# A split user bias, a second layer norm by row factors through DRAM, and another passage and end of a GNN + LSTM kernel

## The reference, cut to what matters

```
xn  = layernorm(x)                                       # first norm, per user
h   = item_feat @ W_item.T + b_item                      # [N, H]
x1  = x + relu(adj @ h + xn @ W_user.T + b_user)         # adj is [N, N], 400 MB
z   = layernorm(x1)                                      # second norm, per user
hs  = LSTM over the N rows of z (one sequence)           # h, c start at zero
g   = argmax(hs @ W_lin.T + b_lin)                       # 0 or 1 per row
w   = g * hs; inc = cumsum(w)
out = x1 + 2*hs + (inc - w)*fw_att + (inc[-1] - inc)*bw_att
```

## Time and profile before

| | |
|---|---|
| median of 3 runs | 1447.24 us (1446.77 to 1447.74) |
| the profiled execution | 1444.94 us, its span 1443.1 us |
| busy share PE / DVE / ACT / POOL | 98% / 86% / 74% / 15% |
| the chain that ended last | PE 91%, DVE 3%, issue 2%, POOL 2%, DMA 1% |
| HBM read / written | 422.42 MB / 10.28 MB |
| stage 1, passage, stage 2, end begin at about | 0, 1136, 1149, 1419 us of the span |

### The profile page before, as it was taken

One profiled execution on the slowest core, in us unless ns is written; L12 is line 12 of the kernel. 1 busy time (PEld: TensorE's weight loads), 2 busy tenths in 40 slices (PEclk: granted clock), 3 DMA queues, 4 the chain that ended last, 5 costly groups with the idle time before them and its releaser, 6 DMA issues.

```text
span 1443.1 us, 26187 instructions
## 1 busy us (share of the span) xinstructions
PE 1412.8 (98%) x7478; PEld 1214.0 (84%) x7478; DVE 1242.8 (86%) x2052; ACT 1067.8 (74%) x1502; POOL 214.5 (15%) x193
## 2 busy tenths in 40 slices
PE   8999999999999999999999999999999899999994
PEld 7878888888888888888888888888888799999993
DVE  7998998998998999999989989989989666676667
ACT  6677777777877877877877877777777576556662
POOL 0000010010001001001001001000000132027775
PEclk9999999999999999999999999999999999999997
DMA  9999999999999999999999999999999203000003
GB/s 374 360 331 357 403 364 370 407 360 362 404 365 364 407 357 364 407 355 377 396 358 387 385 352 401 378 347 403 373 362 400 87 0 142 0 2 0 1 0 143
DMA packets 134877, 433.16 MB, mean 300 GB/s; under 512 B 18683, under 2 KB 35900, under 8 KB 134718
## 3 DMA queue, kind: packets, MB, share of 16 engines
q1 hardware_dynamic: 127776, 426.43, 78.0%
q10 hardware_dynamic: 7070, 6.34, 1.6%
HBM read 422.42 MB, written 10.28 MB: 300 GB/s over the span
## 4 chain that ended last, share of the span: by engine, by line
PE 91%; DVE 3%; issue 2%; POOL 2%; DMA 1%; ACT 0%; POOLq 0%; DVEq 0%; SPq 0%; ACTq 0%
PE psG L842 24%; PE psG L843 24%; PE psG L844 24%; PE psZ L965 8%; PE psZ L951 2%; PE psZ L953 2%; PE psZ L955 2%; PE psG L863 1%; PE psT L810 1%; PE psI L890 1%; DVE a_lo L1130 1%; POOL own L526 1%; PE psZ L971 1%; DMA raw<-in_adj_main 1%; POOL own L529 1%
## 5 line engine op out<-in xcount | busy, mean ns | idle before, releaser
L634 ACT ACTIVATE a_hi<-raw 128x1000 fp32r<-128x1000 f32 (+1 forms) x800 | 821.8, 1031 | 244.8 <-PE psG L844 208.4
L1130 DVE TENSOR_TENSOR a_lo<-raw,a_hi 128x1000 fp32r<-128x1000 f32 (+1 forms) x800 | 911.0, 1170 | 74.5 <-ACT a_hi L634 55.2
L842 PE MATMUL psG<-a_hi,item_hi 128*128 128x500 f32 x1560 | 620.5, 398 | 2.1 <-DVE a_lo L1130 1.1
L843 PE MATMUL psG<-a_lo,item_hi 128*128 128x500 f32 x1560 | 606.0, 388 | 0.0
L844 PE MATMUL psG<-a_hi,item_lo 128*128 128x500 f32 x1560 | 604.7, 388 | 0.0
L842 PEld LDWEIGHTS psG<-a_hi,item_hi 128*128 128x128 f32 x1560 | 293.5, 188 | 66.9 <-issue 5.6
L844 PEld LDWEIGHTS psG<-a_hi,item_lo 128*128 128x128 f32 x1560 | 293.2, 188 | 59.4
L843 PEld LDWEIGHTS psG<-a_lo,item_hi 128*128 128x128 f32 x1560 | 293.6, 188 | 58.6 <-issue 4.4
L452 POOL TENSOR_TENSOR rstd<-var,minus_half 125x4 f32<-125x4 f32 x40 | 76.1, 1902 | 1019.5 <-DVE var L1106 1019.5
L965 PE MATMUL psZ<-hist,wh 128*128 (+1 forms) x1264 | 167.8, 276 | 1.2 <-DVE hist L1304 1.1
L965 PEld LDWEIGHTS psZ<-hist,wh 128*128 128x128 f32 x1264 | 154.9, 192 | 1.7 <-issue 1.6
(11 more groups left out here) (174 smaller groups left out, 769.9 us busy)
## 6 DMA issues: line engine op xcount, KB each, us to landing
raw<-in_adj_main SPq DMA_DIRECT2D x760, 500.0 KB, 6.5
raw<-in_adj_main SPq DMA_DIRECT2D x40, 250.0 KB, 4.5
sq<-rstd_copy ACTq DMA_DIRECT2D x20, 250.0 KB, 7.1
x_copy<-xb SPq DMA_DIRECT2D x20, 250.0 KB, 7.1
u<-x_copy SPq DMA_DIRECT2D x1, 5000.0 KB, 14.4
out<-u SPq DMA_DIRECT2D x25, 200.0 KB, 2.4
u<-in_itemT SPq DMA_DIRECT2D x9, 512.0 KB, 10.1
xb<-in_xT SPq DMA_DIRECT2D x18, 250.0 KB, 5.9
```

The costliest lines, as they stand in the source:

```text
L634: nc.scalar.activation(a_hi[:, s % CUT, 0:n], raw[:, r % RAW, at:at + n], ACT.Copy)\
L842: pe.matmul(bank, w_hi, hi, start=(c == 0), stop=False)
L843: pe.matmul(bank, w_hi, lo, start=False, stop=False)
L1130: last = dve.tensor_tensor(a_lo[:, s % CUT, 0:m], raw[:, r % RAW, at:at + m], a_hi[:, s % CUT, 0:m].bitcast(f32), ALU.subtract)
```

## The change

- **Bias.** `wu` and `v` are split in high and low parts (fp32r); the bias becomes three matmuls like the others. ScalarE makes `v_hi` after piece 4, VectorE `v_lo` after piece 5, TensorE adds the bias after piece 7 (before: after piece 5). In block 0 the bias moves from piece 11 to 13 and the matmuls of `wx` from 12 to 7.
- **Second norm.** `normalise` and `to_columns` go. `add_relu` writes x1 to a buffer of its own, `x1b`, and the rows' 1/std and shift (`row_terms`) go to DRAM after piece 8 (`send_terms`), come back after piece 12 in two broadcasts of 250 KB (`spread_terms`, into `sq` and `un_bb`), and VectorE applies them in place to `x1b` after pieces 16 and 17. `out_u` reads `x1b` and moves from piece 10 to 18.
- **Waits of SP and VectorE.** The next x is loaded without waiting for the store of x1; `add_relu` waits for that store and for `out_u` of the block before.
- **Passage.** Eight matmuls of the identity (`KEEP_WARM`) follow the transposes; the first half of step 1 of the LSTM runs before the transposes back; the input matmuls of step 2 come before the second half of step 1.
- **End.** Two rows of x1 are copied to `x1_last` early; `total` comes before `last_y(1)`; ScalarE makes the shift in PSUM; 13 output parts of 400 to 1000 columns instead of 25; the check follows the last part; POOL's last base sum is issued before its wait for the gate.

```diff
-AT = dict(relu=1, x1=2, scaled=3, bias=5, rows2=3, stats2=4, pair2=5, eps2=5, scale2=6, norm2=7, back2=8, out2=10,
-          rows1=11, stats1=12, pair1=13, eps1=13, send=15, spread=19, store=7, load=10, wx=12)
-FIRST = dict(rows=0, stats=1, send=3, centre=3, centred=4, spread=6, scaled=9, bias=11)
+AT = dict(relu=1, x1=2, scaled=3, v_hi=4, v_lo=5, bias=7, rows2=3, stats2=4, pair2=5, eps2=5, scale2=7, send2=8, spread2=12, apply2=16, shift2=17, out2=18,
+          rows1=11, stats1=12, pair1=13, eps1=13, send=15, spread=19, store=7, load=10)
+FIRST = dict(rows=0, stats=1, send=3, centre=3, centred=4, spread=6, wx=7, scaled=9, v_hi=10, v_lo=11, bias=13)
+OUT_ENDS = (10, 20, 30, 40, 60, 80, 105, 130, 155, 180, 205, 230, K)
+POOL_OUTS = (3, 5, 8, 11)
 (SP)
-                        sp.wait_ge(x1_stored, 16 * j)
-                        sp.wait_ge(ln_rows, 2 * j + 1)
+                        sp.wait_ge(x1_ready, j)
 (ScalarE)
-            def normalise(count):
...
+            def send_terms(j):
+                act.wait_ge(ln_scale, j)
+                act.dma_start(rows_dram.rearrange("k (p s) -> p k s", s=SUB), row_terms[:, :, :])\
+                    .then_inc(terms_stored, 16)
+            def spread_terms(j):
+                act.wait_ge(terms_stored, 16 * j)
+                for k, t in enumerate((factors, rl)):
+                    act.dma_start(t[:, 0:BW], rows_dram[k:k + 1, :].to_broadcast([P, BW])).then_inc(terms_spread, 16)
+            def high_user(j):
+                act.wait_ge(v_ready, j + 1)
+                nc.scalar.activation(v_hi[:, :], v, ACT.Copy).then_inc(v_hi_ready, 1)
...
-                act.wait_ge(ln_back, count)
+                act.wait_ge(ln_applied, 2 * count)
 (TensorE)
-                        pe.wait_ge(v_ready, j + 1)
-                        pe.matmul(bank, wu[:, :], v[:, :], start=False, stop=False)
+                        pe.wait_ge(v_lo_ready, j + 1)
+                        pe.matmul(bank, wu_hi[:, :], v_hi[:, :], start=False, stop=False)
+                        pe.matmul(bank, wu_hi[:, :], v_lo[:, :], start=False, stop=False)
+                        pe.matmul(bank, wu_lo[:, :], v_hi[:, :], start=False, stop=False)
-                    if has2 and r == AT["back2"]:
-                        to_columns(j)
 (TensorE, passage)
+            for _ in range(KEEP_WARM):
+                pe.matmul(psG[:, 1, 0:P], ident[:, :], ident[:, :], start=True, stop=True)
+            from_state(1, 0, 0, 1)
...
             from_input_f32(1, 1, 1)
-            from_state(1, 0, 0, 1)
-            from_state(1, 1, 0, 1)
...
             from_input(LO_ONLY, 2, 0)
+            from_state(1, 1, 0, 1)
 (VectorE)
+            def low_user(j):
+                dve.wait_ge(v_hi_ready, j + 1)
+                dve.tensor_tensor(v_lo[:, :], v, v_hi[:, :].bitcast(f32), ALU.subtract).then_inc(v_lo_ready, 1)
             def add_relu(j):
...
-                dve.tensor_tensor(xb[:, j % 2, :], xb[:, j % 2, :], rl[:, :], ALU.add).then_inc(x1_ready, 1)
+                if not (isinstance(j, int) and j == 0):
+                    dve.wait_ge(x1_stored, 16 * j)
+                    dve.wait_ge(u_ready, j)
+                dve.tensor_tensor(x1b[:, :], xb[:, j % 2, :], rl[:, :], ALU.add).then_inc(x1_ready, 1)
+            def apply_rstd(j):
+                dve.wait_ge(terms_spread, 32 * j)
+                dve.tensor_tensor(by_s(x1b), by_s(x1b), by_r(factors[:, :]), ALU.mult)\
+                    .then_inc(ln_applied, 1)
+            def apply_shift(j):
+                dve.wait_ge(ln_applied, 2 * j - 1)
+                dve.tensor_tensor(by_s(x1b), by_s(x1b), by_r(rl[:, :]), ALU.add)\
+                    .then_inc(ln_applied, 1)
 (VectorE, end)
-            last_y(1)
             dve.wait_ge(cum_ready, 4)
             dve.scalar_tensor_tensor(total[:, :], cum[:, K:K + 1], -1.0, mbw[:, :], ALU.mult, ALU.mult)\
                 .then_inc(total_ready, 1)
+            last_y(1)
```

More of the change, by code:

```diff
@@ L151, in program @@
         xb = sb("xb", [P, 2, BW], f32, first)
-        v = sb("v", [P, BW], f32, first)
-        normed = sb("normed", [P, SUB * HID], f32, first)
+        v_hi = sb("v_hi", [P, BW], f32r, first)
+        v_lo = sb("v_lo", [P, BW], f32r, first)
+        x1_rows = sb("x1_rows", [P, SUB * HID], f32, first)
+        x1b = x1_rows[:, 0:BW]
+        wu = x1_rows[:, 0:HID]
+        item_tail = x1_rows[:, HID:HID + STACKED]
+        normed = x1_rows
         sq = sb("sq", [P, BW], f32, first)
@@ L193, in program @@
         own = sb("own", [P, 2, 2, K])
+        x1_last = sb("x1_last", [P, 2, K])
         x1_head = sb("x1_head", [P, L])
@@ L509, in write_y, with base, sums @@
                 pool.tensor_tensor(rows, own[:, par, :, :], run_c[:, par, :, :], ALU.add).then_inc(y_ready, 1)
-            def sums(i, par, reset=False):
+            def base(i, par):
+                rows = x1[:, :].rearrange("p (k l) -> p l k", l=L)[:, ds(2 * i, 2), :]
+                pool.tensor_tensor(own[:, par, :, :], hist[:, ds(2 * i, 2), :], rows, ALU.add).then_inc(base_ready, 1)
+            def sums(i, par, reset=False, last=False):
+                if last:
+                    pool.wait_ge(h_ready[0], W + 2 * i + 2)
+                    pool.wait_ge(h_ready[1], W + 2 * i + 2)
+                    pool.wait_ge(y_ready, i - 1)
+                    base(i, par)
                 pool.wait_ge(gated, i + 1)
@@ L524, in sums @@
                     write_y(i - 1, 1 - par)
-                rows = x1[:, :].rearrange("p (k l) -> p l k", l=L)[:, ds(2 * i, 2), :]
-                pool.tensor_tensor(own[:, par, :, :], hist[:, ds(2 * i, 2), :], rows, ALU.add).then_inc(base_ready, 1)
+                if not last:
+                    base(i, par)
                 pool.wait_ge(base_ready, i + 1)
@@ L545, in _ @@
                 sums(2 * i + 1, 1)
-            sums(PAIRS - 2, 0)
+            sums(PAIRS - 2, 0, last=True)
             pool.wait_ge(run_c_ready, PAIRS - 1)
@@ L652, in body @@
                         spread_rstd(0)
-                    if has2 and r == AT["norm2"]:
-                        normalise(j)
+                    if r == (FIRST if items else AT)["v_hi"]:
+                        high_user(j)
+                    if has2 and r == AT["send2"]:
+                        send_terms(j)
+                    if has2 and r == AT["spread2"]:
+                        spread_terms(j)
                     if has2 and r == AT["out2"]:
@@ new lines, in first_cell_tanh @@
+            def first_cell_tanh(g):
+                act.wait_ge(c_ready[g], 1)
+                nc.scalar.activation(tb(g, 3), group(C, g), ACT.Tanh, scale=0.5).then_inc(th_ready[g], 1)
+            first_gates(0)
+            first_cell_tanh(0)
+            act.wait_ge(ln_scale, NB)
+            for s in range(2):
+                nc.scalar.activation(normed[0:SW, s * HID:(s + 1) * HID], psT[0:SW, s * HID:(s + 1) * HID],
+                                     ACT.Identity, bias=shift_rows[:, s:s + 1], scale=rstd[:, s:s + 1])\
+                    .then_inc(end_normed_a, 1)
@@ L762, in _ @@
+            act.wait_ge(end_u_v, 1)
+            act.wait_ge(end_u_a, 2)
+            input_hi(1)
+            first_gates(1)
+            cell_tanh(1, 0)
+            first_cell_tanh(1)
+            nc.scalar.activation(slots[:, K - 12:K - 11, HL:L], psT[:, 0:HL].unsqueeze(1), ACT.Copy, bias=1.0)\
+                .then_inc(end_u_a, 1)
             act.wait_ge(special, 2)
             act.wait_ge(dfb_ready, 1)
-            input_hi(1)
-            for r in range(1, 4):
+            gate_pair(1, 1, 0, 1)
@@ L766, in _ @@
+            gate_pair(1, 1, 1, 1)
+            input_hi(2)
+            cell_tanh(1, 1)
+            for r in range(2, 4):
                 lstm(r, r % 2, lambda: input_hi(r + 1))
@@ L778, in _ @@
             lstm_pair(1, 1)
+            act.wait_ge(x1_back, 16)
+            for half in range(2):
+                nc.scalar.activation(x1_last[:, half, :], last_row(x1, L - 2 + half), ACT.Copy).then_inc(x1_last_ready, 1)
             with nc.scalar.Fori(1, PAIRS // 2 - 1) as i:
@@ L784, in _ @@
             act.wait_ge(total_ready, 1)
-            nc.scalar.activation(shift[:, :], cum[:, 0:K], ACT.Identity, scale=dfb[:, 0:1], bias=total[:, 0:1])\
-                .then_inc(shift_sb_ready, 1)
+            for t, done in ((psZ[:, SHIFT_BANK, 0:K], shift_ready), (shift[:, :], shift_sb_ready)):
+                nc.scalar.activation(t, cum[:, 0:K], ACT.Identity, scale=dfb[:, 0:1], bias=total[:, 0:1]).then_inc(done, 1)
             act.wait_ge(flag_ready, 1)
@@ L1338, in _ @@
                               None, ALU.add).then_inc(end_u_v, 1)
+            forget_product(1, 0)
+            input_product(1, 0)
+            cell(1, 0)
             first_cell(1)
+            state(1, 0, 1)
             state(0, 1, 0)
-            for r in range(1, 4):
+            forget_product(1, 1)
+            input_product(1, 1)
+            cell(1, 1)
+            state(1, 1, 1)
```

(1 more changed line is left out.)

314 lines of the change are left out of this document (157 added, 157 removed).

## The result

| | before | changed |
|---|---|---|
| median | 1446.77 us (1445.31 to 1449.90, 7 runs) | 1452.47 us (1450.68 to 1454.03, 7 runs) |
| profiled execution, span | 1444.94, 1443.1 us | 1451.99, 1450.2 us |
| last matmul of stage 1 starts | 1135.64 us | 1148.04 us |
| first output part starts | 1425.53 us | 1434.79 us |

The ratio is 1.0035 (95% interval 1.0022 to 1.0048): slower by 0.35%, where 1440.4 us was forecast. The two parts of the kernel went opposite ways. The stretch behind stage 1 lasts 1443.1 - 1135.64 = 307.5 us before and 1450.2 - 1148.04 = 302.2 after, 5.3 us less (forecast: 5.5). Stage 1 ends 12.4 us later (forecast: 1.3 earlier). Both are read from the two profiled executions, which lie 7.1 us apart; the medians lie 5.7 apart.

The account below looks back on a forecast made before the run. TensorE was taken to bound stage 1, with the DMA stream and VectorE right behind. Stage 1 -1.3, passage -1.5 and end -4.0 made -6.8 us, from 1447.24 to 1440.4 us; own range 1434 to 1444, whole range 1430 to 1451.

Parts of the forecast that it names:

- TensorE's own: Stage 1: shorter bias saves 0.16 us a block and dropped transposes back 0.42, 11.2 us in all.
- wait at piece 6: Stage 1: v_lo delays piece 6's first half while TensorE arrives earlier; 0.42 us a block, 8.0 us in all.
- strided passes and `out_u`: Stage 1, pieces 16 to 18: added VectorE passes and moved `out_u` fit the slack; taken as 0.
- later loads by the broadcasts: Stage 1: added DMA makes loads at piece 2 later by 0.1 us a block, 1.9 us in all.
- Rival 3: Stage 1: strided passes not hidden, pieces 16 to 18 cost 0.45 us a block, 8.6 more: 1447.1 us; chance 0.12.
- Rival 2: Stage 1: loads become the bound, 0.9 us of delay a block, reaching TensorE: 1455.7 us; chance 0.17.
- the room: Stage 1 DMA stream: 1.7 us a block free, so the added 1.3 us fits by 0.2 us.
- Passage and end: Behind stage 1: passage gains 1.5 us, end gains 4.0 us.
- The clock: Passage: identity matmuls keep TensorE from the 1.2 GHz level before step 2; up to 1.4 us.
- the hole: End: gap of about two slices, 1.2 us, in the output stream, which goes as the check follows the parts.
- the flag: End: the check's flag comes at about 1436.7 us; if it ends the program, only 1.9 us is gained.

Follow-up runs that it names:

- e1: Changed kernel with v_lo after piece 6 instead of 5: 1442.71 us; a stall is what a distance above 0.265 us between starts has over 0.226.
- e2: Changed kernel without the two broadcasts of the row terms, only stage 1 read: its last matmul starts at 1150.3 us (whole time 67478 us).
- e4: Kernel before with the second norm's added small stores and two broadcasts, which nobody reads, all compute as before: 1445.39 us.
- e8: e3 plus two unused strided VectorE passes a block after pieces 16 and 17: 1451.17 us.
- e15: e8 with its two unused strided passes after pieces 8 and 9 instead of 16 and 17: 1438.31 us.
- e14: e13 with v_lo after piece 5 instead of 6: 1451.36 us.
- e13: e3 plus only the new bias (split user rows, three passes after piece 7), v_lo after piece 6, old second norm: 1442.26 us.
- e7: e3 plus one unused contiguous VectorE subtraction, as long as v_lo's, after piece 5: 1439.20 us.
- e5: Changed kernel with v_lo after piece 6, broadcasts after piece 11, strided passes after pieces 15 and 16: 1467.48 us.
- e6: e5 with v_hi after piece 5, v_lo after piece 8 and bias passes after piece 9: 1462.83 us.
- e9: Changed kernel with the two strided passes on GpSimd instead of VectorE, v_lo staying after piece 5: 1477.00 us.
- e16: Changed kernel with user rows scaled after piece 7, v_hi after 8, v_lo after 9, bias after 10: 1439.46 us.
- e17: e16 with the strided passes after pieces 15 and 16 instead of 16 and 17: 1440.31 us.
- e3: Kernel before with the changed passage and end alone, stage 1 untouched: 1441.57 us.

## Why the prediction was wrong

By its own steps, for stage 1, in us a block (mean of 19 blocks of the profiled executions, stalls counted as under e1; measured sum 55.94 - 55.33 = +0.61):

| step | forecast | measured |
|---|---|---|
| TensorE's own | -0.58 | three bias passes 0.23 + 0.22 + 0.23 as forecast; the -0.58 fits the sum |
| spacing of the other matmuls | 0 | +0.26 |
| wait at piece 6 | +0.42 | +0.66 (0.47 in short blocks, 0.8 in long ones) |
| strided passes and `out_u` | 0 (0 to 0.9) | +0.24 at the block's start, +0.03 at pieces 2 to 5, and a part of the wait at piece 6 |
| later loads by the broadcasts | +0.10 | 0 (e2, e4) |

The measured terms add up: -0.58 + 0.26 + 0.66 + 0.24 + 0.03 = +0.61. The first block lasts 0.9 us longer too, but over all runs it lasts 84.3 to 87.2 us, so nothing is read from that.

**The step that failed** is "the two strided passes after pieces 16 and 17 come when VectorE has caught up ... I take 0". They cost 9.6 us in a kernel where nothing waits for them (e8), and nothing eight pieces earlier (e15). I weighed them against the slack of the matmuls next to them, and that slack was there: no distance above 0.265 us stands at pieces 16 to 19 in e8. But they also hold back `lo_ready`, and with it the loads of four pieces later, which reach the same run of VectorE that I had called critical at piece 2. In the changed kernel itself their price is read against e14, which has the same bias and no strided passes: 0.23 us more at the block's start, 0.13 at pieces 2 to 5 and 0.15 at piece 6 (0.66 against 0.51), 0.51 us a block or 9.7 us in all, as in e8. Rival 3 named the edit, and its price of 8.6 us is near this; its way (`out_u` behind the shift pass) is the 0.23 us at the block's start, a little less than half.

**The step that was right in kind and short in size** is the wait at piece 6. The 0.42 us were worked out for a block without other delays and were 0.47 there; the mean is 0.66. e1 and e13 to e14 show 9 to 10 us for `v_lo`'s place instead of 8.0. e7 shows that a pass of the same length at the same place costs nothing as long as TensorE still has its bias ahead of piece 6: it took the bias's move to piece 7 as well, as the prediction said.

**TensorE's gain of 11.2 us** was read as a sum that would arrive less the waits, and as far as the starts show, it did. What the forecast lacked is the spacing of all other matmuls, which it took as unchanged. In every kernel with the new bias (the changed one, e1, e2, e5, e6, e9 to e14, e16, e17) the usual distance is 0.2265 to 0.2268 us, in every kernel with the old one (before, e3, e4, e7, e8, e15) 0.2258: 0.18 us a block between the changed kernel and the one before. And the changed kernel has 2.9 starts a block at a distance of 0.254 us or near it (2.1 to 3.4 in the others with the new bias, 0.4 or less in those with the old one), another 0.08. Nearly all are no waits for `a_lo`: before 94% of those in the changed kernel VectorE had ended its last low part 0.24 us earlier or more. With both, 55.22 - 0.58 + 0.26 and the start's 0.24 make 55.14, and the blocks of e1 without another stall last 55.11 to 55.16 us. So nearly half of the 0.58 is eaten. Why was not tried and stays open; the runs tell only that it comes with the edit of the bias (e13 against e3), not which part of that edit makes it.

**Rival 2, the loads**, had 0.17 and the right side (slower) for the wrong reason. ScalarE's queue takes 4.3% of the same 56 us now (1000 to 1056 us), against 1.6%: 2.7% of 56 us, 1.5 us more, near the 1.3 taken. But TensorE, which lost 0.6 us a block elsewhere, gave the stream that room, and even without that (e4, at 387 GB/s) it cost nothing: the forecast's reading that the room holds was right, and its 0.1 us was 0. The rate over whole blocks rose from 377 to 381 GB/s. That is again above the limit of about 358 GB/s for a core that the Trainium skill gives ("DMA: Bandwidth & Descriptors", "Specifications"); the measurement decides, for one core that streams alone.

**Passage and end** were right: -5.3 for -5.5, as -1.1 (-1.5), -2.0 (-2.3) and -2.2 (-1.7). The clock held, the hole went, and the flag is made at 1446.22 while the stream still runs; e3 gives 5.8 us in the medians. That the last term came out larger than taken goes with the faster output stream; packets and hole were not tried apart. What of the passage is the clock's and what the order's was not tried apart.

**The chances.** The result, 1452.47, is outside 1430 to 1451. The case nearest to it is rival 3, with both the wait at piece 6 and the unhidden passes; it had 0.12 and 1447.1 us. What it lacks is the wider spacing, 19 x 0.26 = 4.9 us, which no rival had; so that it comes near is in part luck, since its 0.42 us at piece 6 and its single price for the passes are not where the time stands. It deserved more: the wait at piece 6 was my forecast, and whoever believes VectorE to be full at one place should have doubted my 0 for three times that work at another.

## What to carry to other kernels

An engine that is 91% busy and works in bursts has no average slack. Put added work into the stretch where its own waits stand (here pieces 8 to 11), also when nobody waits for the result, and when a step is moved away from in front of a buffer's user on the bounding engine, look at which engine made that buffer just in time. Follow a late step not only to its readers but to the buffers that it frees: here VectorE's low parts release the loads. And before giving an engine's work to an idle one, measure what the idle one takes from it.
